# Column sums of v from four ones-matmuls instead of VectorE sums of x, and group norm's squares and variance on GpSimd

## What is computed

```python
h = concatenate([patches @ W.T + b, txt], axis=1)            # 8 x 548 x 192
n = layernorm(h); q, k, v = n @ Wq.T, n @ Wk.T, n @ Wv.T     # 3 heads of 64
scores = q . k / 8 * decay        # decay[l, m] = gamma**(m - l) for m >= l, and 0 below
weights = softmax(scores)         # masked entries are scores of 0, not minus infinity
o = weights @ v
o = (o - mean) / sqrt(var + eps)  # group norm per head over all tokens
h = h + (o * gn_weight + gn_bias) @ Wo.T
# then 16 experts of width 128 or 256, the best 8 per token, gelu(x @ w1) @ w2
h = h + moe(layernorm(h))
```

## Time and profile before

| | |
|---|---|
| median of 3 runs | 765.95 us (765.46 to 766.73) |
| the profiled execution, its device time | 763.07 us |
| its span, first to last instruction | 761.3 us |
| TensorE matmuls busy | 719.3 us (94%) |
| TensorE weight loads busy | 605.2 us (79%) |
| VectorE busy | 582.1 us (76%) |
| ScalarE busy | 467.0 us (61%) |
| GpSimd busy | 153.0 us (20%) |
| mean granted clock of TensorE | 0.994 of full speed |

### The profile page before, as it was taken

The page is one execution under the profiler, slowest core; times in us unless marked ns, Lnnn a source line. Parts: engine busy times, 40 slices in busy tenths (PEclk is TensorE's granted clock), DMA queues, the critical chain, the costliest instruction groups (busy, mean ns, idle before and its releaser), DMA issues.

```text
span 761.3 us, 13137 instructions
## 1 busy us (share of the span) xinstructions
PE 719.3 (94%) x4265; PEld 605.2 (79%) x4265; DVE 582.1 (76%) x1616; ACT 467.0 (61%) x1041; POOL 153.0 (20%) x254
## 2 busy tenths in 40 slices
PE   5988999999998799999999999999999999999996
PEld 4777878888986577788888888888888888888895
DVE  7888988998888686677777777767777777677675
ACT  3677778778777646456456456456456456456453
POOL 3062654753543870000000000000000000000000
PEclk9999999999999999999999999999999999999998
DMA  6700011011022651455256255255265255244242
GB/s 196 210 23 22 1 45 44 13 34 44 30 79 65 166 163 45 97 136 128 74 132 128 76 134 125 77 131 132 72 128 136 74 133 121 73 132 94 46 87 43
DMA packets 120564, 70.13 MB, mean 92 GB/s; under 512 B 82000, under 2 KB 100496, under 8 KB 120496
## 3 DMA queue, kind: packets, MB, share of 16 engines
q1 hardware_dynamic: 120496, 69.31, 36.6%
HBM read 58.65 MB, written 10.63 MB: 91 GB/s over the span
## 4 chain that ended last, share of the span: by engine, by line
PE 66%; DVE 21%; ACT 4%; issue 3%; DVEq 3%; DMA 2%; SPq 1%; POOL 0%; POOLq 0%
PE ps L1412 65%; DVE sc L1072 4%; DVE pr L1094 4%; ACT pr L754 2%; DVE nm L1079 2%; DVE k_lo L1035 1%; DVE st L989 1%; DVE gst L1100 1%; DVEq L1077 1%; DVE h L1138 1%; DMA pat<-patches 1%; ACT xa_hi L674 1%; DVE act L1303 1%; DMA gate<-comb_dram 1%; DVE q_lo L1035 1%
## 5 line engine op out<-in xcount | busy, mean ns | idle before, releaser
L884 ACT ACTIVATE act<-ps 128x512 f32<-128x512 f32 (+1 forms) x216 | 124.7, 578 | 205.4 <-PE ps L1412 205.3
L1303 DVE TENSOR_TENSOR act<-act,gate 128x512 f32<-128x512 f32 (+1 forms) x216 | 145.5, 673 | 126.5 <-ACT act L884 117.1
L1412 PE MATMUL ps<-x,w_hi 128*128 128x512 f32 (+1 forms) x648 | 215.2, 387 | 2.2 <-ACT act L884 2.2
L1412 PE MATMUL ps<-x,w_lo 128*128 128x512 f32 (+1 forms) x432 | 165.4, 383 | 0.0
L1035 DVE TENSOR_TENSOR act_lo<-act,act_hi 128x512 fp32r<-128x512 f32 (+1 forms) x216 | 146.1, 676 | 0.2
L1412 PEld LDWEIGHTS ps<-x,w_hi 128*128 128x128 f32 x648 | 120.5, 188 | 27.1 <-ACT act L884 2.7
L674 ACT ACTIVATE act_hi<-act 128x512 fp32r<-128x512 f32 (+1 forms) x216 | 130.2, 603 | 3.2 <-DVE act L1303 3.1
L1412 PEld LDWEIGHTS ps<-x,w_lo 128*128 128x128 f32 x432 | 81.3, 188 | 16.5
L1412 PE MATMUL ps<-act_hi,w_hi 128*128 128x512 f32 (+1 forms) x216 | 83.2, 385 | 3.3 <-DVE act_lo L1035 3.3
L535 POOL TENSOR_TENSOR rstdb<-vepsb,neg_half 128x4 f32<-128x4 f32 x9 | 9.1, 1010 | 379.8 <-DVE vepsb L1168 379.8
L1412 PE MATMUL ps<-act_lo,w_hi 128*128 128x512 f32 (+1 forms) x216 | 83.2, 385 | 0.0
(11 more groups left out here) (183 smaller groups left out, 1200.3 us busy)
## 6 DMA issues: line engine op xcount, KB each, us to landing
gate<-comb_dram SPq DMA_DIRECT2D x128, 256.0 KB, 3.6
w_raw<-w SPq DMA_DIRECT2D x16, 384.0 KB, 3.7
h_dram<-h SPq DMA_DIRECT2D x8, 384.0 KB
res<-h_dram SPq DMA_DIRECT2D x8, 384.0 KB, 3.9
rb<-h_dram SPq DMA_DIRECT2D x48, 64.0 KB, 2.5
out<-rb SPq DMA_DIRECT2D x48, 64.0 KB, 1.9
x_dram<-xn_t SPq DMA_DIRECT2D x24, 96.0 KB, 2.4
gate<-comb_dram SPq DMA_DIRECT2D x16, 144.0 KB, 3.2
```

The source lines that it names most:

```text
L884: a.activation(act[j % 3][:, 0:n], ps[:, up_bank(j), 0:n], ACT.Gelu_apprx_tanh).then_inc(gelu_done, 1)
L1303: dve.tensor_tensor(act[j % 3][:, 0:n], act[j % 3][:, 0:n], gate[e % 4][:, 0:n], ALU.mult).then_inc(gated, 1)
L1412: return pe.matmul(dst, w, x, start=start, stop=stop)
```

## The change

It does four things. (1) The sums of the keys are no longer taken from x: `x_ext` is gone, `xa_hi`, `xa_lo` and `xb` have 548 columns in place of 580, `values` makes 36 rows in its last tile, and the new `value_sums` adds up v over each of the four whole tiles by four matmuls that accumulate (stationary operand `tile_one`, 128x4, a column of ones for tile I; moving operand v, 128x192, both float32). `sums_copy` (ScalarE) copies the result of 4x192 into rows 64 to 67 of v's last tile. (2) In group norm, the square and sum behind the statistics (`gn_squares`) and the variance go to GpSimd, and the copy of the totals from PSUM (`gn_totals`) goes to ScalarE. (3) ScalarE makes the exponentials of head 2's tile 1 ahead of head 1's `pt_copy`. (4) `halve_w1` waits for head 1's scaling in place of head 0's, behind `rstd_of`.

Cut to its core (declarations, imports and the last images' special calls are left out where they only repeat this):

```diff
+def sums_place(b):
+    return (7, 256) if b else (4, 0)
...
-             ("xa_hi", [P, LX], F32R), ("xa_lo", [P, LX], F32R), ("xb", [P, LX], F32R),
+             ("xa_hi", [P, L], F32R), ("xa_lo", [P, L], F32R), ("xb", [P, L], F32R),
...
@@ gpsimd
             def halve_w1(b):
                 pool.wait_ge(ld_w1, nth(b, 16, 16))
-                pool.wait_ge(probs_ready, nth(b, H, 1))
+                pool.wait_ge(probs_ready, nth(b, H, 2))
...
+            def gn_squares(t):
+                pool.wait_ge(gn_stated, nth(t, 1, 1))
+                apart(pool, "pool")
+                pool.tensor_tensor(gtmp[:, :], gmv[:, :, 0], gmv[:, :, 0], ALU.mult)
+                pool.drain()
+                pool.tensor_tensor(gmv[:, :, 1], gmv[:, :, 1], gtmp[:, :], ALU.add).then_inc(gn_part, 1)
+                pool.drain()
...
             def gn_coefficients(t):
-                pool.wait_ge(gn_var, nth(t, 1, 1))
+                pool.wait_ge(gn_read, nth(t, 1, 1))
...
+                pool.tensor_tensor(gsquare[:, :], gtot[:, :, 0], gtot[:, :, 0], ALU.mult)
+                pool.drain()
+                pool.tensor_tensor(gvar[:, :], gtot[:, :, 1], gsquare[:, :], ALU.subtract)
+                pool.drain()
+                pool.tensor_scalar(gvar[:, :], gvar[:, :], 0.0, EPS, ALU.max, ALU.add)
+                pool.drain()
                 pool.tensor_tensor(grstd[:, :], gvar[:, :], neg_half[:, 0:2], ALU.pow)
...
                     norm_next(b + 1)
-                halve_w1(b)
                 if ahead:
                     pool.drain()
                     rstd_of(b + 2, ln1_var, rstd, mv, veps, nmr, ln1_rstd)
+                halve_w1(b)
+                if tail:
+                    gn_squares(b - 1)
@@ scalar
             def x_hi(b, c):
-                a.wait_ge(xt_ext, nth(b, 2, c + 1))
+                a.wait_ge(xt_done, nth(b, 2, c + 1))
...
+            def sums_copy(b):
+                bank, at = sums_place(b)
+                a.wait_ge(vs_done, b + 1)
+                copy(v[SUMS:KEY_LAST, NT - 1, :], ps[0:NT - 1, bank, at:at + V_W]).then_inc(vs_copied, 1)
...
+            def gn_totals(t, bank=GN_BANK):
+                a.wait_ge(gn_sum, nth(t, 1, 1))
+                if t:
+                    a.wait_ge(y_coeff, nth(t - 1, 1, 1))
+                copy(gtot[:, :, :], ps[:, bank, GN_AT:GN_AT + 4].rearrange("p (i k) -> p i k", i=2)).then_inc(gn_read, 1)
...
                 exps(b, 1, (2, 3, 4))
+                sums_copy(b)
                 pt_copy(b, 0)
...
                 if more:
-                    exps(b, 2, (0,))
+                    exps(b, 2, (0, 1))
                     pt_copy(b, 1)
                     o_copy(b, 0, O_BANKS[0])
                     x_hi(b + 1, 0)
                     x_hi(b + 1, 1)
-                    exps(b, 2, (1, 2, 3, 4))
+                    if tail:
+                        gn_totals(t)
+                    exps(b, 2, (2, 3, 4))
@@ vector
-            def x_ext(b):
...
             def gn_partial(t):
...
+                if t < LB:
+                    last.then_inc(gn_stated, 1)
+                    return
                 dve.drain()
                 dve.tensor_tensor(gtmp[:, :], gmv[:, :, 0], gmv[:, :, 0], ALU.mult)
...
-            def gn_variance(t, bank=GN_BANK):
...
                     dve.wait_ge(wo_done, nth(t, 3, i + 1))
+                    if i == 2 and t + 2 < B:
+                        dve.wait_ge(vs_copied, t + 3)
@@ tensor
+            def value_sums(b):
+                bank, at = sums_place(b)
+                pe.wait_ge(v_copied, nth(b, 3, 3))
+                if b == 0:
+                    pe.wait_ge(consts, 4)
+                last = series(ps[0:NT - 1, bank, at:at + V_W], [(tile_one[:, I, :], v[:, I, :]) for I in range(NT - 1)])
+                last.then_inc(vs_done, 1)
...
                 c = slice(hh * HD, hh * HD + HD)
+                if hh == 0:
+                    pe.wait_ge(vs_copied, b + 1)
...
                     project(b - 2, WO_BANKS)
-                pe.wait_ge(v_copied, nth(b, 3, 3))
+                value_sums(b)
+                if not tail:
+                    pe.wait_ge(vs_copied, 1)
                 probs_transpose(b, 0, (0,))
```

More of the change, by code:

```diff
@@ L240, in early_fusion @@
         head_mean = sb("head_mean", [P, P])
+        tile_one = sb("tile_one", [P, NT - 1, NT - 1])
         gnw, gnb = sb("gnw", [P, 2]), sb("gnb", [P, 2])
@@ L282, in early_fusion @@
         ln2_rstd, ln2_normed = sem("ln2_rstd"), sem("ln2_normed")
-        xt_done, xt_ext, xt_hi, xt_lo = sem("xt_done"), sem("xt_ext"), sem("xt_hi"), sem("xt_lo")
+        xt_done, xt_hi, xt_lo = sem("xt_done"), sem("xt_hi"), sem("xt_lo")
+        vs_done, vs_copied, gn_stated = sem("vs_done"), sem("vs_copied"), sem("gn_stated")
         qk_done, qk_hi, qk_lo = sem("qk_done"), sem("qk_hi"), sem("qk_lo")
@@ L289, in early_fusion @@
         o_done, o_copied = sem("o_done"), sem("o_copied")
-        gn_part, gn_sum, gn_var = sem("gn_part"), sem("gn_sum"), sem("gn_var")
+        gn_part, gn_sum, gn_read = sem("gn_part"), sem("gn_sum"), sem("gn_read")
         y_coeff, y_hi, y_lo = sem("y_coeff"), sem("y_hi"), sem("y_lo")
@@ L527, in _ @@
             pool.memset(head_mean[:, :], 0.0)
+            pool.memset(tile_one[:, :, :], 0.0)
+            pool.drain()
+            pool.memset(v[32:SUMS, NT - 1, :], 0.0)
+            pool.drain()
+            for I in range(NT - 1):
+                last = pool.memset(tile_one[:, I, I:I + 1], 1.0)
+            last.then_inc(consts, 1)
             pool.drain()
@@ L717, in x_hi @@
             def x_hi(b, c):
-                a.wait_ge(xt_ext, nth(b, 2, c + 1))
+                a.wait_ge(xt_done, nth(b, 2, c + 1))
                 at = 512 * X_BANKS[c]
-                copy((xa_hi, xb)[c][:, :], psf[:, at:at + LX]).then_inc(xt_hi, 1)
+                copy((xa_hi, xb)[c][:, :], psf[:, at:at + L]).then_inc(xt_hi, 1)
             def two(ap):
@@ L735, in v_copy @@
                         continue
-                    r = P if n == 2 else KEY_LAST
+                    r = P if n == 2 else LAST
                     a.wait_ge(v_done, nth(b, 3, i + 1))
@@ L868, in body @@
                     o_copy(b, 1, LAST_O[1])
+                    gn_totals(t, LAST_GN[t])
             norm_apply(0, rstd, nmr, ln1_rstd, xn, first_normed, range(DVE_TILES, NT))
@@ L905, in beside_first @@
                     y_whole(LB - 1, 1)
+                elif k == 6:
+                    gn_totals(LB, LAST_GN[LB])
                 elif k == 8:
@@ L1038, in two @@
                 return ap.rearrange("p (a n) -> p a n", a=2)
-            def x_ext(b):
-                for i, bank in enumerate(X_BANKS):
-                    dve.wait_ge(xt_done, nth(b, 2, i + 1))
-                    dve.tensor_reduce(ps[:, bank + 1, SUMS:KEY_LAST],
-                                      ps[:, bank, :].rearrange("p (t n) -> p t n", n=P), AX.X, ALU.add).then_inc(xt_ext, 1)
             def x_lo(b, chunks=(0, 1)):
@@ L1051, in x_lo @@
                     if c == 0:
-                        sub(xa_lo[:, :], psf[:, at:at + LX], xa_hi[:, :]).then_inc(xt_lo, 1)
+                        sub(xa_lo[:, :], psf[:, at:at + L], xa_hi[:, :]).then_inc(xt_lo, 1)
                     else:
-                        sub(xb[HD:P, :], psf[HD:P, at:at + LX], xb[HD:P, :]).then_inc(xt_lo, 1)
+                        sub(xb[HD:P, :], psf[HD:P, at:at + L], xb[HD:P, :]).then_inc(xt_lo, 1)
             def qk_rest(b):
@@ L1104, in gn_partial @@
                 gn_stats(t, 1)
+                if t:
+                    dve.wait_ge(gn_sum, nth(t - 1, 1, 1))
                 dve.drain()
                 for i in range(2):
-                    dve.bn_aggr(gmv[:Y_ROWS[i], i, :], gst[:Y_ROWS[i], i, :])
+                    last = dve.bn_aggr(gmv[:Y_ROWS[i], i, :], gst[:Y_ROWS[i], i, :])
+                if t < LB:
+                    last.then_inc(gn_stated, 1)
+                    return
                 dve.drain()
@@ L1280, in body @@
                 if more:
-                    x_ext(b + 1)
                     x_lo(b + 1)
@@ L1288, in body @@
                     router_weights(0)
-                if tail:
-                    gn_variance(t, GN_BANK if more else LAST_GN[t])
                 normalise(b, 2)
-            x_ext(0)
             x_lo(0)
@@ L1491, in values @@
                         I = t0 + i
-                        r = P if I < NT - 1 else KEY_LAST
+                        r = rows(I)
                         c = slice(I * P, I * P + r)
@@ L1603, in x2_transpose @@
                     if t == 1:
-                        pe.wait_ge(gn_var, nth(LB, 1, 1))
+                        pe.wait_ge(gn_read, nth(LB, 1, 1))
                 elif bank == U_BANK:
@@ L1657, in body @@
                     if t:
-                        pe.wait_ge(gn_var, nth(t - 1, 1, 1))
+                        pe.wait_ge(gn_read, nth(t - 1, 1, 1))
                     pe.wait_ge(qk_lo, nth(b, 4, 1))
```

19 lines of the change are left out of this document (5 added, 14 removed).

## The result

The changed kernel takes 770.72 us (median of 6 runs, 769.10 to 773.43) where the kernel before takes 765.81 on the same chip (6 runs, 765.43 to 767.36): a ratio of 1.0066, with a 95% interval of 1.0045 to 1.0087. That is 4.9 us slower, where 3.2 were forecast, and inside the stated range of 766.4 to 772.2. The profiled execution took 773.16 us with a span of 771.3.

What follows compares the result with a forecast made beforehand. TensorE was taken to set the period once its 0.52 us wait for VectorE is gone. Terms -0.7, -1.2, 0, +3.5, +1.4, +0.7, +0.1 and -0.6 make +3.2 on the median 765.95: 769.1 us, range 766.4 to 772.2.

Steps and rivals of the forecast that it cites:

- The sums: `value_sums` on TensorE, between projection and next block: four float32 matmuls of 192 columns add 1.40 us per image.
- Rival 2: The sums on TensorE cost one pass, 0.44 us per image: -2.3 in all, 763.6 us; chance 0.06.
- The covered wait: TensorE's 0.52 us wait before head 1's transposes disappears, so images 2 to 5 pay 0.88 each, not 1.40.
- Rival 3: ScalarE's `pt_copy` of head 1 comes late behind tile 1's exponential: up to 0.5 us in six images, 772.2 us; chance 0.17.
- the cover: Some 0.9 us free between the rounding of x and the first matmul for q, to absorb 0.6 us of lateness.
- The signs: Expected in the trace: 0.8 us before head 2's transposes, VectorE idle 1.3 us before `den`, periods near 28.2, among others.
- Exponentials: Head 2's tiles 2 to 4 on ScalarE start earlier: -0.1 us in each of six images, -0.6 together.
- Start: `x_ext` of image 0 leaves the chain of waits before the first matmuls: -0.7 us.
- Image 0 to 1: Exponentials without tile 1 and x rounded without `x_ext` shorten waits for exponentials and `q_lo`: -1.2 us, at most 1.46.
- Image 6: TensorE has no wait there to cover the added sums: +1.4 us, besides -0.1 for exponentials.
- Image 7: A 0.72 us wait covers half the added sums: +0.7 us; ScalarE's totals copy before its first gelu: +0.1.
- Rival 1: VectorE was the bound and TensorE's blocks have unseen room for the sums: -4.5, 761.4 us; chance 0.08.

Runs made afterwards that it cites:

- experiment 6: Kernel before with only group norm's squares and variance on GpSimd and its totals copied by ScalarE; key sums still from x. 766.67 us, ratio 1.0000.
- experiment 5: Changed kernel with w1's split back behind head 0's scaling and tile 1's exponential behind the rounding of x, ahead of `gn_totals`. 769.14 us, ratio 1.0034.
- experiment 8: Kernel of experiment 6 with w1's split waiting for head 1's scaling from image 1 on. 760.23 us, ratio 0.9941.
- experiment 3: Changed kernel with w1's split waiting for head 0's scaling again. 770.54 us, ratio 1.0059.
- experiment 2: Changed kernel with tile 1's exponential back behind the rounding of x and `gn_totals` behind all four exponentials. 774.89 us, ratio 1.0112.
- experiment 9: Kernel before with only w1's split moved behind head 1's scaling from image 1 on. 762.65 us, ratio 0.9966.

## Why the prediction was right in direction and short in size

**The sums: right.** 1.40 us per image were taken from rows 6 by columns, and 1.40 is what the starts show. Rival 2's price (0.44) is refuted. The Trainium skill's N cycles (TensorE: Matmul & The Clock Gate, Step-by-step) do not hold for this type, since a float32 matmul of 192 columns takes 0.35 us, as rows 6 had said.

**The covered wait: right in size, wrong in its cause.** Its 0.52 us are gone. With w1's split behind head 0 in both, the sums take the period from 27.33 (experiment 6) to 28.19 (experiment 5): +0.86, where 0.88 was forecast. But I put the wait down to VectorE's having too much to do, and it came from 0.84 us of one blocked instruction. Where that is gone first (26.70, experiment 8), the sums cost 1.49, with nothing covered. So the balance per middle image reads, one step after the other: 27.37 before, 27.33 with group norm moved, 28.19 with the sums, 28.72 with ScalarE's late copies (experiment 3), which is the measured +1.35. Part 4, counted at nothing, is worth nothing in this order (experiment 3), but 0.63 per middle image where the sums are not made by TensorE (27.33 to 26.70), and it is the one part that pays by itself.

**Rival 3, given 0.17: it happened.** The late `pt_copy` was priced at up to 0.5 us in six images; experiment 2 measures 0.54 in a middle one. The step of the prediction that failed is the cover: "some 0.9 us are free" between the rounding's end and the first matmul for q. The rows give 0.76 (the rounding of the first half ends 4.14 us after the transposes, the first matmul begins 4.90 after them). And they are for x's first half alone: the rest of its second half ended 0.05 us before its reader. So the first matmul had its room (no wait before it at 159.80), but the fourth pair waited 0.24 for `xb`, and the copies behind `qk` ran on until head 2's `pt` was 0.5 late. I looked for the wait inside `qk` and at head 2's transposes, where 0.8 us of slack took it up; it came out one step further on, in front of the scores, where I had not looked.

**The signs.** Two that I named did not come: head 2's transposes wait 0.28 us and not 0.8, and VectorE waits 0.50 us before `den` and not 1.3. The waits for `xb` and `pt` are of the kind that I had called a sign of being wrong, though neither name stood in my list.

**Exponentials: -0.1 forecast, -0.2 found** at head 2's transposes (S to them 9.91 before, 9.72 after), and lost again behind them, since the scores wait for `pt`.

**Start: -0.7 forecast, -0.25 found** at the first matmul for q (18.66 to 18.41). This point moves by itself: it lies at 18.41, 18.45, 18.59, 18.27, 17.77 and 18.59 in the six profiled executions without `x_ext`, and at 18.66, 18.68, 19.25, 18.70 and 18.37 in the five with it. The means differ by 0.4.

**Image 0 to 1: -1.2 forecast, -1.2 found, by another way.** Head 2's transposes came only 0.4 earlier, not 1.2, because the split held up the scaling (2.80 us). Without that, in experiment 3, it is 1.5, my upper bound, and the whole period is the same 26.96. In the change the other 0.8 came in image 1, where `nm` no longer meets the split. That the number came out is luck: two errors cancelled.

**Image 6: +1.4 - 0.1 forecast, +1.9 found**; the 0.5 is ScalarE's again. **Image 7: +0.7 forecast, +0.55 found**, and nothing for the copy ahead of the gelu.

**Rival 1, that VectorE was the bound, fell twice.** Sums doubled cost 1.3 us per image, and with VectorE's work down by 0.8 the period stayed (27.33). The rule of the Trainium skill's Perfetto Trace Analysis, section Identifying the Most-Contended Engine, which would have started from VectorE's occupancy, leads to the right engine and does not say which of its work counts: 0.8 us fewer changed nothing (experiment 6), and the 0.84 us of one `nm<-mx`, also VectorE's, gave 0.63 (experiment 8). What decided each time was whether the instruction lay in the unbroken run of work before a wait.

**The sum.** The attention stage came out at +6.1, at rival 3's price (+6.2), and not at the forecast's +3.2 or under its own upper edge of +5.0. The medians differ by +4.9; the experts' stage, 510.5 to 514.9 us in eleven traces, can make up the rest, but there is one trace of the kernel before and this is not shown. 770.7 us lies inside the range because the range had been drawn up to rival 3. Its lower end of 766.4 does not follow from the forecast's +1.4, which gives 767.4.

## What to carry to other kernels

A wait names the engine that came last, not the reason: before a wait is put down to the amount of an engine's work, compare each instruction on the way to it with its own kind elsewhere in the trace. One `nm<-mx` of 1.01 us among others of 0.17 was worth more, in the kernel without the ones-matmuls, than the 2.95 us of work that the change took from VectorE. Work moved to the engine that others wait for costs its length less the wait that it fills (1.4 less 0.5 here), while work taken from an engine that waits is given back as more waiting. And what a part is worth depends on the others: the same move of w1's split gave 0.63 us per image without the sums and nothing beside them.

## What the runs showed of the hardware beside this

**VectorE behind GpSimd.** Four kinds of VectorE instruction were lengthened while GpSimd subtracted w1's halves: `nm<-mx` (0.17 to 1.01 us), the five scalings (1.89 to 2.80), the additions of `den` (0.17 to 0.73 and 0.90, in experiment 2) and group norm's square (0.16 to 0.75, in experiment 9). The decay times scores, which reads one operand from PSUM, ran beside the same subtraction unchanged: for 128x292 it took 0.45 us at 148.03 in the kernel before, inside GpSimd's 147.85 to 149.82, and 0.45 in the same image at 143.39.

**The clock after idle time.** The experts' stage begins with TensorE waiting for gates and probabilities, and its granted clock falls there. Busy time by stretch of the kernel after, from the experts' first matmul:

```profile
249.20:255.00 5.80, 3.96 (x16) 2.77 (x15) 4.84 (x31) 2.82 (x11) 4.11 (x8) 0.77 0.07 22
...
260.00:265.00 5.00, 2.04 (x9) 1.55 (x10) 2.97 (x4) 3.59 (x8) 4.57 (x8) 0.75 0.57 194
264.37:268.93 4.56, 4.56 (x10) 3.14 (x11) 1.63 (x2) 0.71 (x2) 4.42 (x7) 0.50 0.49 146
265.00:270.00 5.00, 5.00 (x19) 3.44 (x19) 1.55 (x3) 1.05 (x3) 4.71 (x7) 0.56 0.59 157
270.00:275.00 5.00, 5.00 (x30) 4.04 (x27) 3.47 (x5) 2.47 (x6) 4.10 (x7) 1.00 0.73 238
```

and of the kernel before:

```profile
249.00:255.00 6.00, 3.58 (x13) 2.54 (x13) 2.41 (x6) 3.04 (x7) 5.28 (x11) 0.72 0.73 199
255.00:260.00 5.00, 4.48 (x27) 3.37 (x29) 4.02 (x5) 3.03 (x7) 4.86 (x6) 1.00 0.52 151
```

Before, one stretch is below full speed; after, there are four (255 to 260, not shown, has 0.93), and in 265 to 270 TensorE does 19 matmuls in 5 us at 0.56, mostly at the level of 1.2 GHz, where it does 30 in the next 5 us at 2.4. What preceded is a wait of 2.74 us for ScalarE's transposed probabilities (1.44 in the kernel before). Set beside the kernel before, the 4.0 us by which the experts were longer in this trace fall into three parts: 0.4 up to the transposes at 258.36, 1.4 from there to 264.37, with that wait in it, and 2.2 from 264.37 to 270.85, where the granted clock is 0.50 for most of the time.

Nor is this a matter of the ones-matmuls alone: the stage took 510.5 to 510.6 us in two of the eleven profiled executions, 511.4 to 512.1 in three, and 514.0 to 514.9 in six, the kernel with nothing but group norm moved (514.9) among them. The two short ones are the two kernels with group norm where it was, the kernel before and experiment 9, and image 7's group norm does run in this stage. But both profiled executions are among the fastest of their kernels (763.07 us beside a median of 765.81, 760.05 beside 762.65), so two traces don't tell. Whether the change makes the longer case more frequent was not settled.
